# Quantised feed-forward of a two-layer model: rounded values read as 16-bit integers, peaks spread by TensorE, and the next rounding begun during the up products

## The reference, cut to what matters

```python
def act_qdq(x):
    qmax = 2.0 ** (ACT_BITS - 1) - 1.0
    scale = jnp.maximum(jnp.max(jnp.abs(x)) / qmax, 1e-12)
    return jnp.clip(jnp.round(x / scale), -qmax - 1.0, qmax) * scale

def fixed_qdq_u16(x):
    scale = 1.0 / 65536.0
    return jnp.clip(jnp.round(x / scale), 0.0, 65535.0) * scale
...
x = act_qdq(x)
up = act_qdq(x @ lpbq_dequant(w_up).T)
gate = act_qdq(x @ lpbq_dequant(w_gate).T)
sig = fixed_qdq_u16(jax.nn.sigmoid(gate))
gate = act_qdq(gate * sig)
o = act_qdq(gate * up)
return o @ lpbq_dequant(w_down).T
```

## Time and profile before

| | before |
|---|---|
| median of 3 runs | 1812.0 us (1810.86 to 1813.96) |
| the profiled execution | 1809.76 us, its span 1808.0 us |
| PE busy | 1614.5 us, 89% of the span |
| DVE busy | 1179.7 us, 65% |
| ACT busy | 915.4 us, 51% |
| POOL busy | 800.1 us, 44% |

### The profile page before, as it was taken

How to read it: one execution, slowest core, us unless ns; L and a number is a source line. 1 busy time by engine, 2 the same in 40 slices (tenths; PEclk the granted TensorE clock), 3 DMA queues, 4 the chain that set the end, 5 groups by cost and what they waited for, 6 DMA issues and landing times. The chain is left out here.

```text
span 1808.0 us, 34242 instructions
## 1 busy us (share of the span) xinstructions
PE 1614.5 (89%) x14024; PEld 829.6 (46%) x14024; DVE 1179.7 (65%) x1991; ACT 915.4 (51%) x1261; POOL 800.1 (44%) x406
## 2 busy tenths in 40 slices
PE   5999999999999999986699899898989989699349
PEld 2445555555555555543435543354434444344124
DVE  6588888888888888863555477697312222627881
ACT  1387787877877877764362133311012122228750
POOL 2277887888788888863028234422000000003310
PEclk9999999999999999989799799999999999799779
DMA  3589999999999999996327522243839941000001
GB/s 133 142 151 190 196 190 194 194 191 190 194 192 191 195 188 189 193 167 145 90 76 234 214 74 71 87 132 109 330 125 399 388 180 65 1 1 1 0 1 47
DMA packets 517543, 273.31 MB, mean 151 GB/s; under 512 B 443776, under 2 KB 495488, under 8 KB 514320
## 3 DMA queue, kind: packets, MB, share of 16 engines
q1 hardware_dynamic: 517392, 271.18, 62.5%
HBM read 138.74 MB, written 22.54 MB: 89 GB/s over the span
## 5 line engine op out<-in xcount | busy, mean ns | idle before, releaser
L493 POOL TENSOR_TENSOR x<-x_prob,x 128x1604 bf16<-128x1604 f32 x120 | 388.1, 3234 | 145.5 <-ACT x L648 145.5
L771 DVE TENSOR_REDUCE x_negmax<-x_score 128x1 f32<-128x1604 f32 x128 | 233.6, 1825 | 15.2 <-PE x_score L534 5.1
L630 ACT ACTIVATE x_prob<-x_score,x_negmax 128x1604 f32<-128x1604 f32 x128 | 204.8, 1600 | 44.2 <-DVE x_negmax L771 39.3
L517 PE MATMUL x_ring<-x_ctx_hi,wk_split 128*128 128x400 bf16 (+1 forms) x1024 | 216.2, 333 | 0.3 <-DVE x_kT L707 0.3
L517 PE MATMUL x_ring<-wv_split,x_ctx_hi 128*128 128x512 bf16 (+1 forms) x832 | 214.2, 380 | 0.0
L707 DVE SCALAR_TENSOR_TENSOR x_kT<-x_ring,bk,x_kT 128x400 bf16<-128x400 f32 (+1 forms) x256 | 162.1, 634 | 32.0 <-ACT x_kT L619 24.0
L648 ACT CAST x<-x_prob 128x1604 bf16<-128x1604 f32 x120 | 183.0, 1525 | 0.0
L713 DVE TENSOR_TENSOR x_v<-x_ring,x_v 128x512 bf16<-128x512 f32 (+1 forms) x208 | 143.7, 691 | 52.9 <-ACT x_v L623 50.1
L619 ACT ACTIVATE x_kT<-x_ring,bk 128x400 bf16<-128x400 f32 (+1 forms) x196 | 116.2, 593 | 71.6 <-PE x_ring L517 70.8
L550 PE MATMUL x_pv<-x_pT,x_v 128*64 128x128 bf16 (+1 forms) x3328 | 119.0, 222 | 29.2 <-DVE x_kT L734 17.7
L623 ACT CAST x_v<-x_ring 128x512 bf16<-128x512 f32 (+1 forms) x148 | 86.7, 586 | 97.9 <-PE x_ring L517 97.7
(11 more groups left out here) (330 smaller groups left out, 2595.9 us busy)
## 6 DMA issues: line engine op xcount, KB each, us to landing
y_ctx<-in_ctx SPq DMA_DIRECT2D x16, 1664.0 KB, 10.5
y_ctxT<-in_ctxT SPq DMA_DIRECT2D x16, 1601.0 KB, 14.0
x_stage<-in_ctxT SPq DMA_DIRECT2D x48, 400.0 KB, 4.4
x_q_rows<-q_rows SPq DMA_DIRECT2D x64, 128.0 KB, 3.1
m_xT<-in_L_ffn_w SPq DMA_DIRECT2D x16, 512.0 KB, 4.6
ffn_w_parts<-m_xT SPq DMA_DIRECT2D x32, 256.0 KB, 2.7
x_stage<-in_ctxT SPq DMA_DIRECT2D x16, 401.0 KB, 4.9
f_w<-ffn_w_parts SPq DMA_DIRECT2D x4, 1024.0 KB, 10.6
```

What stands on the lines that cost most here:

```text
L493: pool.tensor_tensor(ph[:, g % 2, 1, 0:NKP], prob[:, g % 2, :], ph[:, g % 2, 0, 0:NKP], ALU.subtract).then_inc(pl_done, 1)
L517: last = pe.matmul(out_, lhs, rhs, start=(i == 0), stop=(i == len(steps) - 1))
L630: nc.scalar.activation(prob[:, g % 2, :].rearrange("p (c n) -> p c n", n=QW), scores, ACT.Exp, bias=nmax[:, g % 2:g % 2 + 1], accum_out=rs ...
L771: dve.tensor_reduce(nmax[:, pair % 2:pair % 2 + 1], scores, mybir.AxisListType.XY, ALU.max, negate=True).then_inc(max_done, 1)
```

## The change

It does these things, all in the feed-forward block:

- **Integer views.** After ROUND is added, the low 16 bits of the fp32 word are the rounded value as a two's complement integer. `whole` views every second 16-bit word of `up` and `gate` as int16, `fraction` does so with `tmp` as uint16. The gate's subtraction (L2226) and the sigmoid's own rounding on ScalarE (L2161) go: the sigmoid reads the integers and applies the unit as its scale, and VectorE's clamp adds ROUND/65536 in the same pass, which rounds to 1/65536. The product of gate and sigmoid is now VectorE's, of two integer views, and no longer GpSimd's. The 12 subtractions for up go too. For the four tiles that GpSimd multiplies later (now 1, 3, 5, 7) ScalarE takes the constant off both silu and up; the other eight are multiplied by VectorE from integer views.
- **Peaks.** The second to fifth peak go through TensorE: it transposes the column of 128 peaks, spread over 128 columns, into PSUM, and VectorE reduces that (`whole_peak`). The first peak stays with GpSimd.
- **Order.** The chain's steps, now 15, are laid on the first eight up tiles (FIRST = 8). The peak of the silu is taken in up tile 8 and spread in tile 9, and ScalarE rounds eight silu tiles among the last three up tiles (SILU), the other four among the up roundings.
- **Start and end.** ScalarE makes four of the eight normalised tiles, as `x * rstd + shift`. The first output tile is rounded, split and multiplied in two halves (HALVES).

The diff, cut to its core:

```diff
+        whole = [a[:].rearrange("p m n -> p (m n)").bitcast(I16).rearrange("p (m n s) -> p m n s", m=MF, s=2)[:, :, :, 0]
+                 for a in (up, gate)]
+        fraction = tmp.rearrange("p a n -> p (a n)").bitcast(U16).rearrange("p (a n s) -> p a n s", a=NB_T, s=2)[:, :, :, 0]
...
-        by_vector = [m for m in range(MF) if m % 3 != 1]
-        by_gpsimd = [m for m in range(MF) if m % 3 == 1]
+        by_gpsimd = [1, 3, 5, 7]
+        by_vector = [m for m in range(MF) if m not in by_gpsimd]
         NB_G = 6
-        STEPS = [range((MF + 4) * m // MF, (MF + 4) * (m + 1) // MF) for m in range(MF)]
+        FIRST = 8
+        STEPS = [range((MF + 3) * m // FIRST, (MF + 3) * (m + 1) // FIRST) if m < FIRST else () for m in range(MF)]
+        SILU = [(), ()] + [()] * (MF - 5) + [range(0, 2), range(2, 5), range(5, 8)]
+        HALVES = [(0, slice(0, 512)), (0, slice(512, TOK))] + [(m, slice(0, TOK)) for m in range(1, MF)]
...
             pool.memset(big[:], ROUND).then_inc(s_big, 1)
+            pool.wait_ge(s_peak, 1)
+            pool.partition_all_reduce(peak[:, 0, 1:2], peak[:, 0, 0:1], P, bass.bass_isa.ReduceOp.max).then_inc(s_all, 1)
             pool.memset(unbig[:], -ROUND).then_inc(s_unbig, 1)
-
-            def spread(n):
-                pool.wait_ge(s_peak, n + 1)
-                pool.partition_all_reduce(peak[:, n, 1:2], peak[:, n, 0:1], P,
-                                          bass.bass_isa.ReduceOp.max).then_inc(s_all, 1)
-
-            for n in range(2):
-                spread(n)
-            for m in range(MF):
-                pool.wait_ge(s_s2, m + 1)
-                pool.tensor_tensor(gate[:, m, :], tmp[:, m % NB_T, :], gate[:, m, :], ALU.mult).then_inc(s_gs, 1)
-            for n in range(2, 4):
-                spread(n)
             for n, m in enumerate(by_gpsimd):
-                pool.wait_ge(s_whole, n + 1)
-                pool.wait_ge(s_u2, m + 1)
+                pool.wait_ge(s_h2w, n + 1)
+                pool.wait_ge(s_u2, n + 1)
                 pool.tensor_tensor(gate[:, m, :], gate[:, m, :], up[:, m, :], ALU.mult).then_inc(s_hp, 1)
...
-            norm.on_tensor(pe)
+            def spread(n):
+                pe.wait_ge(s_peak, n + 1)
+                pe.transpose(banks[0][:, P * (n - 1):P * n], peak[:, n, 0:1].broadcast_to([P, P]),
+                             ident[:]).then_inc(s_spread, 1)
+
+            for t in range(NT):
+                norm.turn_on_tensor(pe, t, (norm.s_hat, t + 1) if t < NT // 2 else (s_hat2, t - NT // 2 + 1))
...
+                if n == half:
+                    spread(1)
+                if n == half + 2 * (FIRST + 1):
+                    spread(2)
+            spread(3)
+            spread(4)
+            pe.wait_ge(s_unit, 13)
             pe.wait_ge(s_w[2], 16)
-            for m in range(MF):
-                pe.wait_ge(s_ol, m + 1)
-                for t in range(NT):
+            for n, (m, at) in enumerate(HALVES):
...
+            act.wait_ge(s_shift, 1)
+            for t in range(NT // 2, NT):
+                nc.scalar.activation(xhat[:, t, :], x[:, t, :], ACT.Identity, bias=shift[:, t:t + 1],
+                                     scale=norm.rstd[:, t, :]).then_inc(s_hat2, 1)
...
-                    act.wait_ge(s_g2, i + 1)
+                    act.wait_ge(s_g1, i + 1)
                     if i >= NB_T:
                         act.wait_ge(s_gs, i - NB_T + 1)
-                    nc.scalar.activation(tmp[:, i % NB_T, :], gate[:, i, :], ACT.Sigmoid).then_inc(s_sg, 1)
-                if 2 <= c <= MF + 1:
-                    i = c - 2
-                    act.wait_ge(s_sg, i + 1)
-                    nc.scalar.activation(tmp[:, i % NB_T, :], tmp[:, i % NB_T, :], ACT.Identity, bias=big[:],
-                                         scale=65536.0).then_inc(s_sr, 1)
-
+                    nc.scalar.activation(tmp[:, i % NB_T, :], whole[1][:, i, :], ACT.Sigmoid,
+                                         scale=unit[:, 1, 0:1]).then_inc(s_sg, 1)
+
+            def silu(m):
+                if m == 0:
+                    act.wait_ge(s_unit, 8)
+                rounded(gate[:, m, :], gate[:, m, :], 2, s_h1)
+                if m in by_gpsimd:
+                    if m == by_gpsimd[0]:
+                        act.wait_ge(s_unbig, 1)
+                    act.wait_ge(s_h1, m + 1)
+                    nc.scalar.activation(gate[:, m, :], gate[:, m, :], ACT.Identity, bias=unbig[:],
+                                         scale=1.0).then_inc(s_h2w, 1)
...
-            act.wait_ge(s_unit, 6)
-            act.wait_ge(s_unbig, 1)
-            for m in range(MF + 1):
-                if m < MF:
-                    rounded(up[:, m, :], up[:, m, :], 2, s_u1)
-                if m == 1:
-                    act.wait_ge(s_unit, 9)
-                if m >= 1:
-                    rounded(gate[:, m - 1, :], gate[:, m - 1, :], 3, s_h1)
-                if m - 1 in by_gpsimd:
-                    act.wait_ge(s_h1, m)
-                    nc.scalar.activation(gate[:, m - 1, :], gate[:, m - 1, :], ACT.Identity, bias=unbig[:],
-                                         scale=1.0).then_inc(s_whole, 1)
-            act.wait_ge(s_unit, 14)
+                for i in SILU[m]:
+                    silu(i)
+            act.wait_ge(s_unit, 10)
             for m in range(MF):
-                rounded(gate[:, m, :], gate[:, m, :], 4, s_o1)
+                rounded(up[:, m, :], up[:, m, :], 3, s_u1)
+                if m in by_gpsimd:
+                    act.wait_ge(s_u1, m + 1)
+                    nc.scalar.activation(up[:, m, :], up[:, m, :], ACT.Identity, bias=unbig[:],
+                                         scale=1.0).then_inc(s_u2, 1)
+                if m >= 2 and m % 2 == 0 and 7 + m // 2 < MF:
+                    silu(7 + m // 2)
+            act.wait_ge(s_unit, 15)
+            for m, at in HALVES:
+                rounded(gate[:, m, at], gate[:, m, at], 4, s_o1)
...
+            def whole_peak(n):
+                dve.wait_ge(s_spread, n)
+                dve.tensor_reduce(peak[:, n, 1:2], banks[0][:, P * (n - 1):P * n], AX, ALU.max).then_inc(s_all, 1)
...
+            norm.small_on_vector(dve)
+            dve.scalar_tensor_tensor(shift[:], norm.meanvar[:, :, 0], -1.0, norm.rstd[:, :, 0], ALU.mult,
+                                     ALU.mult).then_inc(s_shift, 1)
+            norm.hat_on_vector(dve, range(NT // 2))
+            dve.wait_ge(norm.s_hat, NT // 2)
+            for n, done in ((0, norm.s_hat), (1, s_hat2)):
+                dve.wait_ge(done, NT // 2)
+                part = slice(NT // 2 * n, NT // 2 * n + NT // 2)
+                dve.tensor_reduce(amax[:, 0, part], xhat[:, part, :], AX, ALU.max,
+                                  apply_absolute_value=True).then_inc(s_am2, 1)
...
             peak_of(1, amax[:, 1, :])
-            unit_of(1, 3, 1.0)
+            absmax(half)
+            whole_peak(1)
+            unit_of(1, 3)
...
             def chain(c):
-                if c < MF:
-                    dve.wait_ge(s_g1, c + 1)
-                    dve.tensor_scalar(gate[:, c, :], gate[:, c, :], ROUND, unit[:, 1, 0:1], ALU.subtract,
-                                      ALU.mult).then_inc(s_g2, 1)
                 if 2 <= c <= MF + 1:
                     i = c - 2
-                    dve.wait_ge(s_sr, i + 1)
-                    dve.tensor_scalar(tmp[:, i % NB_T, :], tmp[:, i % NB_T, :], ROUND, 65535.0, ALU.subtract,
-                                      ALU.min).then_inc(s_s2, 1)
-                if c >= 4:
-                    i = c - 4
+                    dve.wait_ge(s_sg, i + 1)
+                    dve.tensor_scalar(tmp[:, i % NB_T, :], tmp[:, i % NB_T, :], 65535.0 / 65536.0, ROUND / 65536.0,
+                                      ALU.min, ALU.add).then_inc(s_s2, 1)
+                    dve.wait_ge(s_s2, i + 1)
+                    dve.tensor_tensor(gate[:, i, :], fraction[:, i % NB_T, :], whole[1][:, i, :],
+                                      ALU.mult).then_inc(s_gs, 1)
+                if c >= 3:
+                    i = c - 3
...
-                absmax(half + 2 * m)
-                absmax(half + 2 * m + 1)
-                if m == MF - 1:
-                    dve.wait_ge(s_am, len(groups))
-                    peak_of(2, amax[:, 2, :])
+                for n in (half + 2 * m, half + 2 * m + 1):
+                    if n > half:
+                        absmax(n)
+                    if n == half + 2 * FIRST + 1:
+                        dve.wait_ge(s_am2, 2 + MF)
+                        peak_of(2, amax[:, 2, 0:MF])
+                    if n == half + 2 * (FIRST + 1):
+                        whole_peak(2)
...
+            dve.wait_ge(s_am, len(groups))
+            peak_of(3, amax[:, 3, :])
+            whole_peak(3)
+            unit_of(3, 9)
...
+            for n, m in enumerate(by_vector):
+                dve.wait_ge(s_h1, m + 1)
+                dve.wait_ge(s_u1, m + 1)
```

(52 more changed lines are left out.)

84 lines of the change are left out of this document (38 added, 46 removed).

## The result

The changed kernel takes **1804.92 us** as the median of 7 runs (1803.0 to 1806.15), the kernel before beside it 1810.86 (7 runs, 1809.9 to 1813.96): a ratio of 0.9965, 95% interval 0.9953 to 0.9976. It is faster by 6 us, more than the 0.2% that can be told from none. I had forecast no change. The profiled execution took 1804.92 us, its span 1803.2.

A forecast was written before the change was run, and what follows sets the result against it. The prediction took TensorE's up products and the 52 us without TensorE behind them as the bound. Terms -1.6 + 11.5 - 7.2 - 1.1 - 1.5 = +0.1 us gave a median of 1812 us; range 1804 to 1818.

The forecast's parts named there:

- start of the block, to the first product: Norm at the block's start: four of eight normalised tiles go to ScalarE, -1.6 us.
- TensorE's wait: In the up products, TensorE waits 10.6 us behind group 19 for VectorE's peak, then runs at low clock.
- start of the up rounding, both rows above in it: Rounding of up behind the up products: +11.5 us, with the block's start at -1.6.
- between up and down, up rounding to last peak pass: Between up and down products: VectorE decides, 30.4 us against 37.6 before, -7.2 us.
- four holds by GpSimd's products: Between up and down: VectorE passes wait for GpSimd's four products, 1.1 us each, 4.4 us together.
- peak exchange to output rounding: Ahead of the output rounding: the peak goes through TensorE in 1.6 us against 2.7, -1.1 us.
- first half tile: Output rounding to first down product: half a tile takes 1.9 us against 3.4, -1.5 us.
- all of the block: Feed-forward block: all terms together +0.1 us, no change that can be measured.
- integer product: VectorE's product of two 16-bit integer views takes 1.22 us, as the fp32 product does.
- the fast integer product: Rival: VectorE's integer product takes 0.6 us, -8 us, 1804 us in all; chance 8%.
- the cheaper wait: Rival: TensorE's wait costs less (clock up at once, no GpSimd holds, lighter exchanges), 1808 us or less; chance 22%.
- a product of 2.2 us: Rival: VectorE's integer product is slow; at 2.2 us it is +16, 1828 us; chance 12%.

The follow-up runs named there:

- small parts undone: Changed kernel with all normalised tiles on VectorE, output peak by all-reduce, first output tile whole, small GpSimd product at the end: 1808.82 us, spread 1804.18 to 1816.57.
- three kernels on GpSimd's end: Kernel before with a small GpSimd product last: 1805.46 us; changed kernel with a spare all-reduce last: 1810.51; changed kernel with all-reduce, then product: 1805.11.
- the kernel before with the quick start: Kernel before with one small GpSimd product added behind its last all-reduce: 1805.46 us, ratio 0.9955 to the kernel before.
- the rescheduled version: Changed kernel with all products on VectorE, sigmoid chain over ten up tiles, later silu peak transposition, small GpSimd product last: 1789.22 us, ratio 0.9882 to the kernel before.

## Why the prediction was wrong

By its own steps, counted inside the block:

| step | forecast | measured | where |
|---|---|---|---|
| start of the block, to the first product | -1.6 | -1.2; -1.6 in six other profiles with the same start; 1.7 when undone | changed, small parts undone |
| TensorE's wait | 10.6 | 10.37 | changed |
| start of the up rounding, both rows above in it | +9.9 | +10.0 (160.3 us behind `g_rstd`, 150.3 before) | changed |
| between up and down, up rounding to last peak pass | 30.4 | 30.4 | changed |
| of it, four holds by GpSimd's products | 4.4 | 4.3 (1.05 to 1.14 each) | changed |
| peak exchange to output rounding | 1.6 | 1.7 | changed |
| first half tile | 1.9 | 2.15 | changed |
| all of the block | +0.1 | +0.6 | both |
| integer product | 1.22 | 1.22 | changed |
| the start of the program | 0 (no term) | -6.1 at the first copy, -5.5 at the block; 5.4 to 6.7 in the time | changed, three kernels on GpSimd's end |

Every term of the sum held to half a microsecond, and the block alone gives the forecast: the kernel before with the quick start takes 1805.46 us, the changed one 1804.92. The step that failed stands in no line of the sum. It is the assumption under it, that the program ahead of the block stays as it is, since no code of it changes. I had counted GpSimd's all-reduces only for what they cost where they stand. The 10.48 us of "issue" at GpSimd's start was in the trace of before; I did not look outside the block, and so did not ask what that wait depends on. Of the rivals that gave 1808 or less, the fast integer product did not happen, and the cheaper wait neither: the wait cost its price. That the time fell inside the range, near the end that the fast product was to give, is luck: none of the range's reasons brought it there. A slip in the rivals changes nothing: at its own price of 1.5 us for each 0.1, a product of 2.2 us costs 14.7 us and not 16. The hold was read loosely from the earlier trace rows (VectorE's pass ends 0.55 us behind GpSimd's there, not just behind it), but its size came out.

That the change doesn't pay in its block is right as well: its shorter tail (from the up rounding to the first down product 34.3 us instead of 43.6) was paid for ahead of it (+10.0), and that price was mostly one of order. With only the work taken away (no product on GpSimd, eight ScalarE passes less) the up rounding starts 156.89 us behind `g_rstd`; with the order changed too, in the rescheduled version, 142.46, against 160.27 in the changed kernel.

## What to carry to other kernels

When a change adds or takes away GpSimd's last instruction of a kind, compare the two traces from 0 and not from the changed line; in this program one small product at GpSimd's end, where a memset did not do it, was worth 5.4 to 6.7 us an execution. Judge other parts by the time alone only when both kernels begin alike, since here a block 3.4 us faster looked 3 us slower. A wait put into the middle of TensorE's products cost what VectorE's queue was behind, and half the clock for 4.4 us on top, so spread that queue's work evenly first and place the wait then.

## What the hardware showed that I had not expected

- GpSimd's first AFFINE_SELECT at 1.5 us or at 11 to 11.5, by what GpSimd did last, 60 us and more before the program's end (250 us in the kernel without GpSimd products). A memset doesn't count.
- Behind an all-reduce a product of one column starts only 7.0 to 7.7 us later (five kernels), a memset at once.
- VectorE passes of 8 columns took 1.2 to 1.9 us instead of 0.17 beside GpSimd's constants (a memset of 1.79 us and passes of 2 us), one-input passes among them (L129, 1.26 us).
- An all-reduce of one column takes 0.72 us from peak to use when GpSimd had 11 us to get ready, and 1.84 us where the peak came 4.3 us after GpSimd's last product.
- VectorE's integer product beside a GpSimd product of 2.35 us ends about 1.1 us behind it (2.27 us instead of 1.22), so four products given to GpSimd saved VectorE 0.5 us in all.
- After gaps of 1.8 and 3.2 us TensorE's granted clock was still 1.00; after 10.37 us it was half for 4.4 us.
